# Decoder chain on GpSimd: slices of 32 features, products placed between the links, level masks on VectorE

## The chip, the core and the metric

One core of a Trainium2 chip runs the whole program. The metric is the device time in microseconds of one execution; 16 iterations of one loop follow a prologue. Engines: PE is TensorE, DVE is VectorE, ACT is ScalarE, POOL is GpSimd, SP is SyncE and issues DMAs.

## What is computed

Two decoder layers over x of (64, 128, 256): a gated delta-rule attention, cross attention and a mixture of 4 experts, then latent attention, cross attention and a mixture of 8 experts. What the change touches is the start of the first one, whose decays need a very exact sum over the features:

```python
log_decay = -exp(A_log) * softplus(einsum('btd,hd->bth', x, W_alpha) + dt_bias)   # x: normalised rows
cum = cumsum(log_decay, -1)
L_mask = tril(exp(tril(cum[..., :, None] - cum[..., None, :])))
M = tril(-(wk_scaled @ wk.T) * L_mask, -1)
A = solve_triangular(eye - M, eye, lower=True, unit_diagonal=True)   # per head, block of 128
```

The kernel forms the sum over 256 features as products with their rounding errors and adds them in a fixed order with an exact two-sum. It forms A by blockwise inversion in seven levels: at each level a mask picks the blocks of M that join two halves.

## The kernel before

**Tiling.** An iteration handles G = 4 sequences of 128 tokens, tokens on the 128 partitions; two heads (DH). `NIT` = 16 iterations run on each engine in a loop of its own, ordered by semaphores that count; the order on each engine is written out by hand.

**The chain on POOL.** The feature chain of the *next* iteration's rows (`xn_next`) is formed by `chain_products` (L394) and `chain_links` (L419). Features are cut in four slices of 64. Per slice come 22 products (128x256 elements each: high and low parts, their products and error terms, into `sp_p` and `sp_e`), then 16 rounds of 4 features (LANES). A round is eight small links on 128x32 elements, acc_a, acc_b, acc_c, acc_d, acc_c, acc_c, acc_c, acc_s, six of which wait for the link just before them; acc_d needs no wait and the acc_c behind it waits for an earlier one. `link` (L631) counts them in `chain_step`. One place for products serves all slices, so a slice's products start when the last slice's links are over.

**What else stands in POOL's order** (L627 to L682): among the products of slice 0 the twelve level masks (`lev`, L647, 128x512; from level 3 on each waits for the product W of two levels before), the residual add of xn0 (L652, `xin_used`, after it SP moves the next rows), 5 rounds, the bias add (L656), which waits for the layer norm's `xn`, a wait for DVE's root (`ref_step`), 11 rounds, slice 1, 5 rounds, the add of onb_row (L663), a wait for the router's gates (`g_w`), and all the rest. Before the last 8 rounds it waits for `x_norm`; then `chain_step` reaches CHAIN_READ and SP moves x_in to xn_next and loads the rows after next. The chain ends with `au` (L678). POOL then centres those rows (`centered`, L506), waits for `y_ready`, squares them and adds the first 16 of 32 groups of squares (`first_squares`, L523), and forms `decay_table` (L533), which the next iteration's MT needs.

**On DVE.** The loop (L1732) begins with two copies and the last 16 additions of squares (`exact_squares`, L1418), in pieces between the levels of the inversion (Um += U, L1823); then `exact_variance`. After attention(0) comes the mixture of 4 experts (e = 0 to 4), with the router and pieces of the exact normalisation of the rows after next in between, attention(1), attention(2), and the mixture of 8. In attention a unit u is a max over the scores (L1854) and a subtraction (L1858); ACT forms the exponential (L804), PE transposes and multiplies. The decay is worked out in steps of 8 to 10 numbers per partition (`decay_exponential`, parts 0 to 9, L1507): part 0 waits for `au`. Parts 0 to 4 (17 steps) stand before the third output block of attention(2) (b == 2, unit 17), parts 5 to 7 (10 steps) before the fourth, parts 8 and 9 after `xT_copy(5)`. At the end `first_level` (L1634) forms MT and the first level for the next iteration.

**The prologue** runs the chain of the first rows split: POOL forms all products (four places, `slice_pe`), DVE the links, and POOL then sums and normalises the second rows, waiting for DVE's root of them, which stands in DVE's links of slice 3 (L1710).

## Time and profile before

| | us |
|---|---|
| median of 3 runs (lowest, highest) | 5413.46 (5405.54, 5415.52) |
| the profiled execution, its span | 5405.82, 5403.9 |
| PE busy | 4731.9 (88%) |
| DVE busy | 4303.5 (80%) |
| POOL busy | 3938.4 (73%) |
| ACT busy | 2323.7 (43%) |
| one iteration (middle of the trace, 2525 to 2845 us) | 320.0, PE 293.4, DVE 255.3, POOL 236.0 |

Times in rows are us from the start of the span. A timeline row is start, duration, engine, line, what it writes from what, and in brackets the idle time of its engine before it with what ended that. `x5` merges five instructions. L635 is a helper: all links and products of the loop stand under it, L563 those of the prologue, L503 the row sums.

### The profile page before, as it was taken

Reading aid. Unit: us, or ns where it says so; the run is one execution under the profiler, and the core shown is the slowest. Engines: PE = TensorE matmul, PEld = TensorE weight load, DVE = VectorE, ACT = ScalarE, POOL = GpSimd, SP = SyncE. Lnnn points to the kernel's source line nnn. Section 1 sums busy time; section 2 is a strip of 40 time slices with the busy share of each in tenths; the row PEclk is TensorE's granted clock in tenths of the full one; section 3 lists DMA queues with packets and bytes.
Section 4 is the critical chain, followed back from the end, with each engine's and each line's share of the span. In section 5 each row is a group of like instructions: output and inputs, shape, how many; then the busy total and the mean of one; then the engine's idle time right before and its main releaser. Section 6 shows DMA issues by size and latency. Waiting matters only on the chain.

```text
span 5403.9 us, 105986 instructions
## 1 busy us (share of the span) xinstructions
PE 4731.9 (88%) x28362; PEld 3086.5 (57%) x28362; DVE 4303.5 (80%) x11377; ACT 2323.7 (43%) x4480; POOL 3938.4 (73%) x10789
## 2 busy tenths in 40 slices
PE   1089999999999999999999999998999999899999
PEld 0065656656565565656556565664656556565655
DVE  8878788787878877787877778777787887878788
ACT  0044444454444444443444544445444444444444
POOL 7478686777868678686767868676785867778686
PEclk7599999999999999999999999999999999999999
DMA  3000000000000000000000000000000000000000
GB/s 89 8 13 9 21 1 25 5 9 21 1 29 1 25 5 9 21 1 29 1 13 17 9 21 1 25 5 9 21 9 21 1 25 5 9 21 1 21 1 17
DMA packets 61894, 78.20 MB, mean 14 GB/s; under 512 B 11168, under 2 KB 53808, under 8 KB 61232
## 3 DMA queue, kind: packets, MB, share of 16 engines
q1 hardware_dynamic: 52784, 62.42, 3.6%
q10 hardware_dynamic: 8448, 8.39, 0.4%
q8 instruction: 240, 3.93, 0.3%
q14 instruction: 422, 3.46, 0.2%
HBM read 45.04 MB, written 8.46 MB: 10 GB/s over the span
## 4 chain that ended last, share of the span: by engine, by line
PE 33%; POOL 29%; DVE 21%; issue 11%; ACT 4%; POOLq 2%; DMA 0%; DVEq 0%; ACTq 0%; SPq 0%
POOL acc_c L635 11%; POOL arena L635 6%; PE bank L1331 3%; PE bank L1238 3%; POOL acc_a L635 3%; POOL acc_b L635 3%; POOL acc_s L635 3%; POOL sl_t L635 2%; PE bank L1191 2%; DVE arena L2088 2%; PE bank L1067 2%; POOLq L634 2%; PE bank L1074 2%; PE bank L1157 2%; PE bank L1143 2%
## 5 line engine op out<-in xcount | busy, mean ns | idle before, releaser
L1854 DVE TENSOR_REDUCE smax<-bank 128x4 f32<-128x512 f32 x768 | 525.2, 684 | 92.3 <-PE bank L1149 51.0
L817 ACT ACTIVATE arena<-bank 128x512 f32<-128x512 f32 x768 | 454.9, 592 | 249.4 <-PE bank L1157 243.7
L1858 DVE TENSOR_TENSOR arena<-bank,smax 128x512 f32<-128x512 f32 x768 | 531.2, 692 | 26.4
L1157 PE MATMUL bank<-ident,arena 128*128 128x128 f32 x3072 | 485.8, 281 | 43.0 <-ACT arena L804 25.7
L1238 PE MATMUL bank<-w,arena 128*128 128x512 f32 x1024 | 490.4, 610 | 14.0 <-DVE arena L1806 14.0
L1143 PE MATMUL bank<-arena 64*128 64x512 f32 x1536 | 440.2, 650 | 64.4 <-ACT arena L841 28.0
L1157 PEld LDWEIGHTS bank<-ident,arena 128*128 128x128 f32 x3072 | 346.9, 141 | 242.9 <-ACT arena L806 82.2
L1271 PE MATMUL bank<-w,arena 128*128 128x256 f32 x2048 | 454.1, 380 | 13.9 <-ACT arena L876 13.9
L804 ACT ACTIVATE arena<-arena,rstd 128x512 f32<-128x512 f32 x512 | 368.1, 719 | 197.9 <-DVE arena L1858 193.4
L1271 PEld LDWEIGHTS bank<-w,arena 128*128 128x128 f32 x2048 | 387.8, 190 | 90.3 <-issue 23.0
L635 POOL TENSOR_TENSOR acc_a<-acc_s,arena 128x32 f32<-128x32 f32 x1008 | 262.1, 260 | 175.4 <-DVE gate L1973 51.8
L876 ACT ACTIVATE arena<-bank,lnb,lng 128x512 f32<-128x512 f32 x256 | 197.3, 777 | 442.1 <-PE bank L1256 439.3
L1169 PE MATMUL bank<-arena 128*32 128x128 f32 x6144 | 327.5, 285 | 57.1 <-ACT arena L810 54.5
L949 PE MATMUL bank<-causal,identb 128*128 128x512 bf16 x658 | 158.5, 380 | 201.9 <-DVE y_nat L1596 198.9
L635 POOL TENSOR_TENSOR acc_c<-acc_a,acc_b 128x32 f32<-128x32 f32 x1008 | 265.7, 264 | 79.7
L635 POOL TENSOR_TENSOR acc_s<-acc_a,acc_c 128x32 f32<-128x32 f32 x1008 | 266.0, 264 | 78.9
L635 POOL TENSOR_TENSOR acc_c<-acc_c,arena 128x32 f32<-128x32 f32 x1008 | 264.4, 262 | 78.8
L635 POOL TENSOR_TENSOR acc_b<-acc_a,acc_s 128x32 f32<-128x32 f32 x1008 | 264.0, 262 | 78.8
L635 POOL TENSOR_TENSOR acc_c<-acc_c,acc_d 128x32 f32<-128x32 f32 x1008 | 262.5, 260 | 78.9
L503 POOL TENSOR_TENSOR arena<-arena 128x1024 f32<-128x1024 f32 x17 | 32.2, 1893 | 394.2 <-DVE y_nat L1596 394.1
L635 POOL TENSOR_TENSOR arena<-arena,sl_t 128x256 f32<-128x256 f32 x384 | 289.2, 753 | 27.6
L647 POOL TENSOR_TENSOR arena<-arena,levmask 128x512 f32<-128x512 f32 x192 | 239.8, 1275 | 65.6 <-DVE arena L1643 65.6
(437 smaller groups left out, 11962.0 us busy)
## 6 DMA issues: line engine op xcount, KB each, us to landing
arena<-in_x_dram SPq DMA_DIRECT2D x35, 512.0 KB, 3.6
xn_next<-arena SPq DMA_DIRECT2D x17, 512.0 KB, 2.9
arena<-cum_dram SPq DMA_DIRECT2D x17, 512.0 KB, 3.8
arena<-in_ctx_dram SPq DMA_DIRECT2D x16, 512.0 KB, 3.7
out_dram<-arena ACTq DMA_DIRECT2D x16, 512.0 KB, 3.1
xn<-xn_next SPq DMA_DIRECT2D x15, 512.0 KB, 3.0
w<-in_L_ffn_w_dram SPq DMA_DIRECT2D x8, 512.0 KB
w<-in_L_ffn_w_dram SPq DMA_DIRECT2D x1, 1024.0 KB
```

Source lines behind the costliest of these rows:

```text
L635: operation(*operands).then_inc(chain_step, 1)
L647: pool.tensor_tensor(heads(lev[:, l % 2, h, :]), heads(MT[:, h, :]), levmask[:, l, :].unsqueeze(1).broadcast_to([P, G, P]), ALU.mult).then ...
L804: act.activation(Ssb[:, v % 4], Ssb[:, v % 4], ACT.Exp, scale=rstd[:, v // 4:v // 4 + 1]).then_inc(S["p_exp"], 1)
L817: act.activation(PT[:, v % 2], bank[3 + v % 2][:, :].rearrange("p (h q) -> p h q", h=QH), ACT.Copy).then_inc(S["pt"], 1)
L876: act.activation(zT[:, e % 2, k, :], bank[4 + n % 2][:, :], ACT.Relu, scale=lng[:, e, k:k + 1], bias=lnb[:, e, k:k + 1]).then_inc(S["zT"], 1)
L1143: ins = mm(bank[S_BANKS[v % 4]][:, :], QT[rows, c, g * P:(g + 1) * P], KM[rows, g, min(c, chunks - 1)].rearrange("p h t -> p (h t)"), star ...
L1157: ins = tr(bank[3 + v % 2][:, j * P:(j + 1) * P], Ssb[:, v % 4, j, :], ident[:, :])
L1169: ins = mm(bank[5][2 * HD * j:2 * HD * (j + 1), (v % 4) * P:(v % 4 + 1) * P], V2[:, g, (v % 4) * QH + j, :], PT[:, v % 2, j, :], start=Tru ...
L1238: ins = mm(bank[g][:, :], xT[:, c, g * P:(g + 1) * P], w1_0[:, e, c, :], start=(c == 0), stop=(c == C - 1))
L1271: ins = mm(bank[6 + g // 2][:, (g % 2) * D:(g % 2 + 1) * D], zT[:, e % 2, k, g * P:(g + 1) * P], w2_0[:, e, k, :], start=(k == 0), stop=(k ...
L1854: dve.tensor_reduce(smax[:, u, :], sc, AX, ALU.max).then_inc(S["s_max"], 1)
L1858: dve.tensor_tensor(Ssb[:, u % 4], sc, smax[:, u, :].unsqueeze(2).broadcast_to([P, QH, P]), ALU.subtract).then_inc(S["s_sub"], 1)
```

## The change

Slices have 32 features, so there are eight, each with 22 products of 128x128 elements and 8 rounds. Two sets of product places (`sp`) alternate, and the products of slice j + 1 are issued one by one between the links of slice j, at three places of each round. Only the 22 products of slice 0 stand alone. Waits count links and products apart. The twelve level masks go to DVE: four and two copies at the start, the masks of level l + 2 behind the add of level l. The 16 additions of squares go from DVE to POOL, behind `decay_table` (`second_squares`). Parts 0 to 3 of the decay's exponential stand behind units 12 to 15 of attention(2), parts 4 and 5 before block 2, parts 6 to 8 before block 3. POOL's waits stand at other rounds. In the prologue POOL forms eight slices of products, DVE eight of links, with its inserted work at the same rounds as before.

```diff
-SLICE = 64
+SLICE = 32
-        sp_p = unit(24, 0, DH * G * SLICE).rearrange("p (h b d) -> p h b d", b=G, d=SLICE)
-        sp_e = unit(24, DH * G * SLICE, DH * G * SLICE).rearrange("p (h b d) -> p h b d", b=G, d=SLICE)
+        sp = [[half_slice(24, 2 * m), half_slice(24, 2 * m + 1)] for m in range(2)]
+        slice_pe = [[half_slice(u, 2 * m), half_slice(u, 2 * m + 1)] for u in (24, 7, 9, 0) for m in range(2)]
...
                 link(tt, acc_a[:, :, :], acc_s[:, :, :], pj, ALU.add)
+                if between:
+                    between()
                 link(tt, acc_b[:, :, :], acc_a[:, :, :], acc_s[:, :, :], ALU.subtract)
                 link(tt, acc_c[:, :, :], acc_a[:, :, :], acc_b[:, :, :], ALU.subtract)
                 link(tt, acc_d[:, :, :], pj, acc_b[:, :, :], ALU.subtract, known=True)
                 link(tt, acc_c[:, :, :], acc_s[:, :, :], acc_c[:, :, :], ALU.subtract, behind=1)
+                if between:
+                    between()
                 link(tt, acc_c[:, :, :], acc_c[:, :, :], acc_d[:, :, :], ALU.add)
                 link(tt, acc_c[:, :, :], acc_c[:, :, :], ej, ALU.add)
+                if between:
+                    between()
                 link(tt, acc_s[:, :, :], acc_a[:, :, :], acc_c[:, :, :], ALU.add)
...
+            def second_squares(it, a):
+                w8 = sq.rearrange("p b (k n) -> p b k n", n=32)
+                for k in range(16, 32):
+                    sum_link(it, a, pool.tensor_tensor, lan2[:, :, :], lan2[:, :, :], w8[:, :, :, k], ALU.add)
...
+                def counted(operation, operands, after):
+                    if after > 0:
+                        pool.wait_ge(chain_step, nth(it, CHAIN_STEPS, after))
+                    operation(*operands).then_inc(chain_step, 1)
+                    count["all"] += 1
+                def rounds(first, last):
+                    for n in range(first, last):
+                        j, k = divmod(n, SLICE // LANES)
+                        def next_product():
+                            if j + 1 < SLICES and count["next"] < PRODUCTS:
+                                chain_products(pool, product, src, j + 1, sp[(j + 1) % 2], count["next"], count["next"] + 1)
+                                count["next"] += 1
+                        if k == 0:
+                            count["next"] = 0
+                            count["link"] = count["product"] = count["all"]
+                        chain_links(pool, link, j, k, k + 1, sp[j % 2], next_product)
+                        if j == 0 and k + 1 == SLICE // LANES:
+                            next_product()
...
-                for l in range(1, LEVELS):
-                    chain_products(pool, link, src, 0, LEVEL_PRODUCTS[l - 1], LEVEL_PRODUCTS[l])
...
+                chain_products(pool, product, src, 0, sp[0])
+                rounds(0, INPUT_ROUND)
...
-                chain_links(pool, link, 0, 0, 5)
+                rounds(INPUT_ROUND, NORM_ROUND)
...
-                chain_links(pool, link, 0, 5, 16)
-                chain_products(pool, link, src, 1)
-                chain_links(pool, link, 1, 0, ROUTER_LINKS)
+                rounds(NORM_ROUND, ROUTER_ROUND)
...
-                chain_links(pool, link, 1, ROUTER_LINKS, 16)
...
+                rounds(ROUTER_ROUND, READ_ROUND)
                 pool.wait_ge(x_norm, nth(it, 1, 1, 2))
-                chain_links(pool, link, 3, 8, 16)
+                rounds(READ_ROUND, SLICES * SLICE // LANES)
...
                 decay_table(it, 1)
+                second_squares(it, 1)
...
-                xT_copy(0)
+                level_mask(1, 0)
                 wait("ctx_psum", 2)
                 dve.tensor_copy(ctxT[:, 1, :], bank[3][:, :]).then_inc(S["ctxT_dve"], 1)
-                dve.wait_ge(sum_step, nth(it, SUM_STEPS, SUM_STEPS))
-                exact_squares(16, 21)
+                level_mask(1, 1)
+                xT_copy(0)
+                for h in range(DH):
+                    level_mask(2, h)
...
+                    if l + 2 < LEVELS:
+                        for h in range(DH):
+                            level_mask(l + 2, h)
...
-                        exact_squares(21, 25)
...
-                        exact_squares(29, 32)
+                        dve.wait_ge(sum_step, nth(it, SUM_STEPS, SUM_STEPS))
                         exact_variance()
...
+                            if a_no == 2 and 12 <= u:
+                                decay_exponential(u - 12)
...
                             if a_no == 2 and b == 2:
-                                for part in range(5):
-                                    decay_exponential(part)
+                                decay_exponential(4)
+                                decay_exponential(5)
                             if a_no == 2 and b == 3:
-                                for part in range(5, 8):
+                                for part in range(6, 9):
                                     decay_exponential(part)
...
                 xT_copy(5)
-                decay_exponential(8)
...
+INPUT_ROUND = 6
+NORM_ROUND = 9
+ROUTER_ROUND = 25
+READ_ROUND = 58
-CHAIN_READ = 530
+CHAIN_READ = 640
-CHAIN_STEPS = 594
+CHAIN_STEPS = 682
```

## Rows read from the trace of the kernel before

**Rows 1.** the chain of work that ended last, share of the span by engine
```profile
PE 33%; POOL 29%; DVE 21%; issue 11%; ACT 4%; POOLq 2%; DMA 0%; DVEq 0%; ACTq 0%; SPq 0%
```

**Rows 2.** waits: who waited for whom, us in total, times, longest
```profile
POOL arena L503 <- DVE y_nat L1596: 394.1, 16, 26.7
```

**Rows 3.** line L1511, what ended DVE's idle time before it: us, times
```profile
  POOL au L678: 16.7, 13
```

**Rows 4.** timeline of POOL, the first link after the gates
```profile
2641.41 0.25 POOL L635 TENSOR_TENSOR acc_a<-acc_s,arena 128x32 f32<-128x32 f32 x1 [3.24 <-DVE gate L1973]
```

**Rows 5.** timeline of POOL, links from 2580 us, then 22 products, then links
```profile
2580.39 0.25 POOL L635 TENSOR_TENSOR acc_a<-acc_s,arena 128x32 f32<-128x32 f32 x1 [2.96 <-DVE row L1398]
...
2581.26 0.25 POOL L635 TENSOR_TENSOR acc_d<-arena,acc_b 128x32 f32<-128x32 f32 x1
2581.47 0.25 POOL L635 TENSOR_TENSOR acc_c<-acc_s,acc_c 128x32 f32<-128x32 f32 x1
...
2606.76 0.61 POOL L635 TENSOR_TENSOR sl_t<-xn_next,splitter 128x256 f32<-128x256 f32 x1
...
2623.88 0.26 POOL L635 TENSOR_TENSOR acc_a<-acc_s,arena 128x32 f32<-128x32 f32 x1
```

**Rows 6.** POOL by line and shape: count | busy us, mean ns | idle
```profile
L472 POOL TENSOR_TENSOR levmask<-arena 128x128 f32<-128x128 f32 x7 | 3.2, 453 | 0.6
...
L635 POOL TENSOR_TENSOR arena<-arena,sl_t 128x256 f32<-128x256 f32 x384 | 289.2, 753 | 27.6
...
L647 POOL TENSOR_TENSOR arena<-arena,levmask 128x512 f32<-128x512 f32 x192 | 239.8, 1275 | 65.6 <-DVE arena L1643 65.6
...
L503 POOL TENSOR_TENSOR lan<-lan,arena 128x32 f32<-128x32 f32 x238 | 64.3, 270 | 18.6
```

**Rows 7.** timeline at the start of an iteration
```profile
2517.89 0.61 POOL L635 TENSOR_TENSOR sl_t<-xn_next,splitter 128x256 f32<-128x256 f32 x1
...
2522.70 0.69 DVE L1641 TENSOR_TENSOR arena<-arena,levmask 128x512 f32<-128x512 f32 x1
...
2527.97 4.68 DVE L1425 TENSOR_TENSOR lan<-lan,arena 128x32 f32<-128x32 f32 x5
...
2532.78 1.29 DVE L1823 TENSOR_TENSOR arena<-arena,bank 128x512 f32<-128x512 f32 x2
...
2533.52 1.25 PE L1089 MATMUL bank<-ident,arena 128*128 128x128 f32 x8 [0.51 <-DVE arena L1823]
...
2575.09 2.35 POOL L656 TENSOR_TENSOR arena<-arena,bo_row 128x1024 f32<-128x1024 f32 x1 [8.20 <-DVE arena L1802]
```

**Rows 8.** timeline at the end of attention(2): start, us, engine, line [idle before]
```profile
2779.49 0.69 DVE L1854 TENSOR_REDUCE smax<-bank 128x4 f32<-128x512 f32 x1 [0.81 <-PE bank L1149]
...
2786.78 0.20 POOL L678 TENSOR_TENSOR au<-acc_a 128x8 f32<-128x8 f32 x1
...
2787.01 0.27 DVE L1511 TENSOR_TENSOR dec_t<-au,a_row 128x8 f32<-128x8 f32 x1 [0.86 <-POOL au L678]
...
2787.72 0.74 ACT L804 ACTIVATE arena<-arena,rstd 128x512 f32<-128x512 f32 x1
...
2788.80 0.66 PE L1178 MATMUL bank<-ident,arena 128*128 128x128 f32 x4
...
2790.82 0.26 DVE L1875 RECIPROCAL orec<-bank 128x16 f32<-128x16 f32 x1
```

**Rows 9.** timeline of DVE, three steps beside work of POOL
```profile
2635.99 2.21 DVE L1927 TENSOR_TENSOR arena<-arena,lt_mask 128x16 f32<-128x16 f32 x1
...
2685.90 1.10 DVE L1398 TENSOR_TENSOR arena<-arena 128x512 f32<-128x512 f32 x1
...
2714.16 0.48 DVE L1474 SCALAR_TENSOR_TENSOR arena<-arena,row 128x256 f32<-128x256 f32 x1
```

**Rows 10.** timeline of the prologue, DVE's first link and POOL's second quotient
```profile
70.83 0.65 DVE L1700 TENSOR_TENSOR acc_s<-arena 128x32 f32<-128x32 f32 x1 [6.95 <-POOL arena L563]
...
192.04 1.90 POOL L563 TENSOR_TENSOR arena<-arena,row 128x1024 f32<-128x1024 f32 x1 [42.81 <-DVE row L1398]
```

## What the change should do to the time

> **What bounds the kernel now.** The chain that ended last is shared: POOL 29%, PE 33%, DVE 21% [rows 1]. So I read next who waits for POOL. Of its 16 iterations (320 us each) POOL itself idles long, 394.1 us for y_nat [rows 2], which is slack: it has nothing to do until attention(2) has left its buffers. What it delivers late is `au`, the end of the feature chain: DVE stood idle for it 16.7 us in 13 places, 1.04 us per iteration [rows 3]. Before that, POOL waits 3.24 us for the gates [rows 4]. So the loop runs gates, 145 us of POOL, `au`, tail of attention(2); the path through PE and DVE is only about 1 us shorter. However fast POOL gets, that little is what an iteration can return there. The rest of the question is what moves onto DVE, and the prologue.
>
> **POOL's chain, step by step.** A round of eight links takes (2606.76 - 2580.39)/11 = 2.40 us: two steps of 0.21 us and six of 0.33 [rows 5]. The step from acc_d to the next acc_c has a wait on an earlier link and still takes 0.21, so a wait that is already met costs nothing; 0.12 us is what a link pays for waiting on the link just before it. A block of 22 products takes 2623.88 - 2606.76 = 17.1 us [rows 5]. For the half-size product the trace has a 128x128 tensor_tensor of 453 ns on POOL, against 753 ns for 128x256 [rows 6]; I take 0.46. Put between two dependent links it costs 0.21 + 0.41 - 0.33 = 0.29 us net (bounds: 0.21, if its start also hides, and 0.54, its whole length with a wait of its own of 0.08). All 176 instead of 88 products: 22 in one block at about 0.52 = 11.4 us, 154 between links at 0.29 = 45 us, together 56 against 68 us. The twelve level masks leave POOL: 12 x 1.25 = 15 us [rows 6]. Sixteen additions for the squares come, 16 x (0.27 + 0.08 for the wait) = 5.5 us [rows 6], behind `decay_table`.
>
> The waits between cut this into pieces. (1) Start to bias add: POOL comes to the chain at 2517.9 [rows 7]; squares 5.5, products 11.4, the round of one link, five rounds of 3.27, the residual add 2.4, three rounds 9.8 give 2563.4; with DVE's own masks in its way (12 x 0.5 us, first level 2) 2571. The bias add can't start before 2575.1 [rows 7], so all of this gain is idle time. The residual add is over at about 2562, before DVE asks for it at 2566. (2) From 2580.4 to the gates: 16 rounds x 2.40 + 44 x 0.29 = 51 us against 55.4; POOL waits some 4 us longer. (3) From the gates, 2641.4 [rows 4]: 39 rounds x 2.40 + 85 x 0.29 = 118 us, and 6 us of collisions as now (now 43 x 2.40 + 2 x 17.1 = 137.4 worked out, 145.1 measured): `au` at about 2767 instead of 2786.8 [rows 8]. x_norm, for which POOL waits in round 58, is written at the end of attention(1), about 2743, and POOL gets there at about 2750: no wait. move_next and load_x come with it, 7 us for both before `centered`, about as long as the 12 us that are left.
>
> **What that returns.** DVE now asks for `au` after unit 12, at 2780.9 (its max of that unit starts at 2779.49, 0.69 + 0.72 us [rows 8]): 14 us of slack. Of the decay steps (17 in 2790.82 - 2787.01 [rows 8], 0.21 us each) 13 move into units 12 to 15: 0.8 + 3 x 0.6 us. The last subtraction ends at 2787.8 instead of 2786.15, while its exponential starts at 2787.72 now [rows 8]: hidden but for 0.1 to 0.3. Behind them DVE has 8 steps instead of 17: it reaches the reciprocal at 2788.4 + 1.65 = 2790.05 instead of 2790.82, and PE has delivered by 2789.4 [rows 8]. That is 0.77 us, with the mean wait (1.04, here 0.86) **0.95 us** per iteration. After it PE and DVE take turns, nothing of POOL. The step that leaves the place behind xT_copy(5) (0.6 us) lies beside PE's expert matmuls: nothing.
>
> **Masks on DVE.** 12 x 0.69 us replace 16 squares of 0.66 to 1.2 (five in 4.68 [rows 7]): in 40 us, DVE isn't fuller. In level 1 the squares kept DVE until 2532.78 from adding U, which PE had ready at 2531.1; PE took its next transposes at 2533.52, having been free from 2532.9 [rows 7]: **-0.6 us**. In the later levels the two masks (1.4 us, waiting for nothing) and the decay product fit well into 5.9 us. But POOL used to stand still while DVE formed the first level, and now runs squares and products: three of its four ops on SBUF alone wait for a product each, about 0.2, **+0.6 us** on the path.
>
> **Two engines on one memory path.** This is the unknown term. A DVE gate op of 0.16 us took 2.21 us beside POOL's 2.37 us add; a subtraction of the masks' shape, which take 0.69 [rows 7], took 1.10 beside 128x256 products; a step of 0.48 us beside links took 0.48, nothing more [rows 9]. Products held DVE up, links did not. The product blocks stood at fixed places; now a quarter of the time until 2751 is products, each of half the length. On the path I count: mixture_norm 8 ops, **+0.5**; attention(1), where DVE runs without a gap, 8 ops, **+0.3**; small steps of the norms, **+0.2**; and e == 3, whose block goes, **-0.5** (DVE was 2.9 us longer there, but PE delivers only 0.5 us before). Together +0.5; bounds: -0.5 (no op waits) and +3 (20 ops on the path at 0.14, a third of those 0.41: the duty and length of the new products). The Trainium skill, SBUF — State Buffer, section "SBUF: two separate sides", says that the pair of ports is locked for the whole instruction and that the loser blocks fully. The 2.21 us agree; the 0.48 us beside links that run 0.25 of every 0.33 us do not. By that rule every POOL op would hold DVE, and the loop would lose nearer the upper bound.
>
> **Prologue.** DVE's chain begins when the first 22 products are there: 53.7 + 11.3 = 65.0 instead of 70.83 [rows 10]. Beside products it does two ops per POOL op; 16 rounds in 53.6 us now, and 37 in 85 us with the short ones. POOL's sums then end at 175 instead of 149, but it waited 42.81 us for DVE's root [rows 10], which comes at 184: **-7.9 us** (bounds -10 and 0). All behind it moves along.
>
> **Sum.** Per iteration -0.95 - 0.6 + 0.6 + 0.5 = -0.45; 16 x -0.45 - 7.9 = -15 us. The profiled execution took 5405.8 (span 5403.9), so 5391 by its own time; the median of the three runs is 5413.5, 0.14% above, and I give the time on its level: **5398 us**.
>
> **Rivals.** *Collisions are light* (0.13): as beside links, no DVE op waits. Then -0.95 - 0.6 - 0.5 = -2.05 per iteration, -33 - 8 us: 5372. For it: the 0.48 rows. *The tail gives nothing* (0.17): PE or ACT is as late as DVE, the added steps in units 12 to 15 eat the 0.95: +0.5 x 16 - 8: 5414. For it: the moved subtraction ends 0.1 us after the exponential's present start. *Collisions decide, slower* (0.14): DVE ops between 2517 and 2750 wait for interleaved products with +3 instead of +0.5 per iteration: -0.45 + 2.5 = +2.05, +33 - 8: 5438. It decides from 1.0 us of added waiting per iteration. For it: 1.10 against 0.69. *The products don't hide* (0.06): at 0.54 net each, `au` comes at 2787, DVE stands at unit 12 for 6.2 us of which 2 have slack: +4.2 x 16: 5465. It begins to hurt at 0.29 + 14/85 = 0.45 us net. Against it: the met wait at 0.21.
>
> **Chances.** My forecast 0.50, its own range 5385 to 5411. About 0.2% (11 us) is what a measurement of this kernel tells from no change. Faster: two thirds of the forecast, all of the first rival, 0.02 of the second: 0.48. Slower: most of the third and all of the fourth: 0.19. Same: 0.33. Range: 5372 to 5430, leaving out half of the third rival, the fourth and a rest below.
>
> **What would show it.** DVE's wait for `au` gone, POOL's last link at about -20 us against attention(2); rounds of 3.27 us with three products; POOL's waits for y_nat near 44 us per iteration, for the gates 7 and for the bias add larger; the add of U in level 1 directly behind PE; DVE's root in the prologue at 184. Wrong, if two-input DVE ops in attention(1) or mixture_norm are longer than 0.48 by more than 0.1 in the mean, if the first level takes over 1 us more, or if the tail between the last score and the reciprocal is not shorter.

## The result, and the profile after

| | before | after |
|---|---|---|
| median (lowest, highest), us | 5414.49 (5405.54, 5416.1) | 5361.07 (5358.8, 5361.5) |
| ratio of the medians, 95% interval | | 0.9903 (0.9888, 0.9918) |
| profiled execution, its span | 5405.82, 5403.9 | 5361.46, 5359.7 |
| mean granted clock of TensorE, of full speed | .954 | .961 |
| first iteration starts at | 281.7 | 274.2 |
| one iteration, mean of 16 | 319.86 | 317.56 |

The change makes the kernel 0.97% faster, 53 us. I had forecast 5398 us, with a range down to 5372: the direction was right, the size too small and the range too narrow.

The page of after, busy time by engine and the chain that ended last:

```profile
PE 4697.3 (88%) x28362; PEld 3072.0 (57%) x28362; DVE 4119.1 (77%) x11313; ACT 2322.5 (43%) x4480; POOL 3977.9 (74%) x12365
...
PE 62%; DVE 22%; issue 8%; ACT 6%; SPq 1%; POOL 1%; DVEq 0%; DMA 0%; ACTq 0%; POOLq 0%
```

POOL stood on the chain with 29% [rows 1] and has 1% of it now. PE executes the same 28362 matmuls in 34.6 us less (4731.9 before): the same work at a higher clock. That is the first sign of what the forecast had left out. The waits of after (who waited for whom, us in total, times, longest):

```profile
POOL arena L509 <- DVE y_nat L1622: 664.7, 16, 42.4
POOL acc_a L648 <- DVE gate L2011: 103.5, 16, 6.5
...
POOL arena L689 <- DVE arena L1828: 49.2, 16, 4.1
```

POOL waits 41.5 us per iteration for y_nat where it waited 24.6 [rows 2], and 6.5 for the gates where it waited 3.24 [rows 4]. Nobody waits for `au` any more; its last link comes 19.2 us earlier in the iteration. To see where the time went I took, in both traces, the start of some twenty instructions relative to the start of DVE's first level (L1639 in before, L1665 in after, where the forming of MT begins), and averaged over the 16 iterations. The last mixture norm is its last op, layer norm 5 its first add, attention(1) and attention(2) their first max over scores. Per stretch, after minus before, beside what the sum had said:

| stretch of an iteration | forecast, us | measured, us |
|---|---|---|
| start to attention(0): first level, inversion | 0.0 | -0.61 |
| to the last mixture norm: attention(0), router, experts | +0.2 | +2.0 |
| to the first score of attention(1) | 0.0 | -1.8 |
| attention(1) to attention(2) | +0.3 | +0.2 |
| attention(2) to layer norm 5 | -0.95 | -1.84 |
| mixture of 8 to the end | 0.0 | -0.2 |
| sum | -0.45 | -2.3 |

Two stretches that the forecast had at about nothing moved by 2 us in opposite directions, and the tail returned twice what it should.

**The tail: the clock.** PE's timeline around block 2 of attention(2), in two iterations of before (start, duration, engine and line, what it writes from what; in brackets its idle time before it), the seventh first, and then PE's busy time and granted clock (the column behind the count) in 8 us that hold the block:

```profile
2470.60 0.44 PE L1199 MATMUL bank<-ident,arena 128*128 128x128 f32 x2 [1.54 <-DVE arena L1877]
...
2471.32 1.36 PE L1191 MATMUL bank<-wo,arena 128*128 128x256 f32 x4
2472.48 1.06 PE L1178 MATMUL bank<-ident,arena 128*128 128x128 f32 x4
```

```profile
1509.52 0.44 PE L1199 MATMUL bank<-ident,arena 128*128 128x128 f32 x2 [0.34 <-DVE arena L1877]
...
1510.24 1.13 PE L1191 MATMUL bank<-wo,arena 128*128 128x256 f32 x4
1511.21 0.60 PE L1178 MATMUL bank<-ident,arena 128*128 128x128 f32 x4
```

```profile
2469.20:2477.20 8.00, 6.60 (x32) 0.79 0.01 3
```

```profile
1507.20:1515.20 8.00, 7.65 (x62) 1.00 0.02 5
```

The same iteration of after, PE's timeline and the window of all engines (PE, PEld, DVE, ACT, POOL, clock):

```profile
2449.35 0.44 PE L1225 MATMUL bank<-ident,arena 128*128 128x128 f32 x2 [0.47 <-DVE arena L1915]
...
2450.07 1.13 PE L1217 MATMUL bank<-wo,arena 128*128 128x256 f32 x4
2451.04 0.60 PE L1204 MATMUL bank<-ident,arena 128*128 128x128 f32 x4
```

```profile
2448.60:2456.60 8.00, 7.52 (x50) 4.88 (x45) 6.23 (x27) 2.51 (x7) 0.00 (x0) 1.00 0.01 4
```

Behind an idle stretch of 1.54 us four transposes take 1.06 us, behind 0.34 and 0.47 us they take 0.60. TensorE has fallen from its full 2.4 GHz to 1.2 GHz for part of the block. Over the 16 iterations of before PE's gap ahead of this block is between 0.34 and 2.81 us. The clock of the 8 us that hold the block is .79 in eight iterations, those with a gap of 1.5 us or more (one of 1.56 us kept 1.00), and 1.00 in the rest. In after the gap is 0.46 to 0.49 and the clock 1.00 in all 16. So the wait for `au` [rows 3] had a second price, which no wait row shows: the slower matmuls after it. The Trainium skill, TensorE: Matmul & The Clock Gate, section "Part 1: The HAM clock gate (the "warmup" mystery)", says that a monitor halves the array's clock when the engine has been idle; the rows agree that the clock falls behind idle time, and of the monitor they show nothing.

**The mixture: collisions lose 2 us, the clock gives 1.8 back.** DVE's groups by line and shape, count | busy us, mean ns | idle; first before, then after:

```profile
L1474 DVE SCALAR_TENSOR_TENSOR arena<-arena,row 128x256 f32<-128x256 f32 x272 | 139.6, 513 | 5.1
...
L1466 DVE TENSOR_SCALAR arena<-arena,row 128x256 f32<-128x256 f32 x68 | 37.0, 585 | 0.1
...
L1984 DVE SCALAR_TENSOR_TENSOR arena<-arena,rstd 128x256 f32<-128x256 f32 x64 | 27.8, 473 | 0.0
```

```profile
L1500 DVE SCALAR_TENSOR_TENSOR arena<-arena,row 128x256 f32<-128x256 f32 x272 | 154.4, 568 | 5.1
...
L2022 DVE SCALAR_TENSOR_TENSOR arena<-arena,rstd 128x256 f32<-128x256 f32 x64 | 33.3, 560 | 0.0
...
L1492 DVE TENSOR_SCALAR arena<-arena,row 128x256 f32<-128x256 f32 x68 | 23.4, 385 | 0.1
```

The ops that met a 17 us block of products got shorter without it (L1466 585 ns, L1492 385). They are the quotient behind expert 3, two per iteration, 378 instead of 821 ns, and what DVE saves there it spends waiting for PE (L2048, 53.9 us in total; the same op waited 2.4 us for PE in before); the two behind expert 1 didn't change (378 and 397 ns). Other ops got longer. The eight steps of the quotient's rest behind expert 1 (L1474, now L1500) take 576 instead of 495 ns in the mean, 0.65 us per iteration, and DVE's z of expert 2, for which PE waits, comes 1.0 us later. The last op of the mixture norm, L1984, has become L2022 and takes 560 instead of 473 ns, four times per iteration. PE's wait for z, before and then after:

```profile
PE bank L1256 <- DVE arena L1998: 36.6, 21, 2.2
```

```profile
PE bank L1282 <- DVE arena L2036: 52.6, 32, 2.2
```

What PE's clock did in the 20 us around the end of the mixture, the eighth and the seventh iteration, before and then after (busy us, clock):

```profile
2692.00:2712.00 20.00, 15.46 (x73) 0.91 0.01 2
2371.20:2391.20 20.00, 15.74 (x73) 0.89 0.01 2
```

```profile
2668.20:2688.20 20.00, 15.16 (x79) 1.00 0.00 1
2350.60:2370.60 20.00, 15.16 (x78) 0.97 0.01 1
```

The mean over the 16 iterations is .871 before and .974 after. PE's idle stretches there are not shorter in after (it stood 1.02 us before L1020 in the eighth iteration of before, and 1.32 us before the same transposes in after), so this is a gain whose cause I can't name; more below.

### The profile page after: what moved, and what is told of

Its sections match the earlier page's. It is cut to its first block, busy times and chain, and to the rows that moved or that the text cites. A ratio compares the mean times of both kernels' runs of the same rounds, so it can differ in the third digit from the quotient of the medians.

```text
span 5359.7 us, 108430 instructions
## 1 busy us (share of the span) xinstructions
PE 4697.3 (88%) x28362; PEld 3072.0 (57%) x28362; DVE 4119.1 (77%) x11313; ACT 2322.5 (43%) x4480; POOL 3977.9 (74%) x12365
## 4 chain that ended last, share of the span: by engine, by line
PE 62%; DVE 22%; issue 8%; ACT 6%; SPq 1%; POOL 1%; DVEq 0%; DMA 0%; ACTq 0%; POOLq 0%
PE bank L1264 7%; PE bank L1297 5%; PE bank L1357 5%; PE bank L1183 5%; PE bank L1169 4%; PE bank L1383 3%; PE bank L1195 3%; PE bank L1217 3%; PE bank L1093 3%; DVE smax L1890 3%; PE bank L1100 3%; DVE arena L1500 2%; PE bank L1282 2%; ACT arena L856 2%; PE bank L1175 2%
## 5 line engine op out<-in xcount | busy, mean ns | idle before, releaser
L648 POOL TENSOR_TENSOR acc_a<-acc_s,arena 128x32 f32<-128x32 f32 x1008 | 273.2, 271 | 225.9 <-DVE gate L2011 103.5
L1297 PEld LDWEIGHTS bank<-w,arena 128*128 128x128 f32 x2048 | 387.8, 190 | 90.3 <-issue 23.0
L648 POOL TENSOR_TENSOR arena<-arena,sl_t 128x128 f32<-128x128 f32 x768 | 361.3, 470 | 9.7
L648 POOL TENSOR_TENSOR acc_b<-acc_a,acc_s 128x32 f32<-128x32 f32 x1008 | 288.9, 287 | 10.0
L1264 PEld LDWEIGHTS bank<-w,arena 128*128 128x128 f32 x1024 | 185.6, 198 | 170.9 <-issue 153.6
L509 POOL TENSOR_TENSOR lan<-lan,arena 128x32 f32<-128x32 f32 (+1 forms) x748 | 237.6, 318 | 57.2
```

The lines of the kernel that those rows point to most:

```text
L509: operation(*operands).then_inc(sum_step, 1)
L648: operation(*operands).then_inc(chain_step, 1)
L1264: ins = mm(bank[g][:, :], xT[:, c, g * P:(g + 1) * P], w1_0[:, e, c, :], start=(c == 0), stop=(c == C - 1))
L1297: ins = mm(bank[6 + g // 2][:, (g % 2) * D:(g % 2 + 1) * D], zT[:, e % 2, k, g * P:(g + 1) * P], w2_0[:, e, k, :], start=(k == 0), stop=(k ...
```

## The experiments

Each run was timed beside the kernel before. Offsets are means over 16 iterations from the start of the iteration, as above; "clock" is the granted clock of a stretch, a mean over 16 windows (170 to 190 us and 268 to 276 us of each iteration). `keep_busy(n, bank)` issues n matmuls whose result nobody reads.

| kernel | median, us | last mixture norm | attention(1) | `au` | layer norm 5 | iteration | clock, end of mixture | clock, block 2 |
|---|---|---|---|---|---|---|---|---|
| before | 5414.5 | 176.06 | 189.53 | 264.85 | 274.04 | 319.86 | .871 | .893 |
| after | 5361.1 | 177.44 | 189.09 | 245.62 | 271.94 | 317.56 | .974 | 1.00 |
| b_fill_tail | 5393.2 | 175.88 | 189.65 | 264.88 | 273.63 | 319.13 | .867 | 1.00 |
| b_fill_mix | 5421.3 | 176.07 | 187.53 | 264.77 | 274.57 | 320.99 | 1.00 | .751 |
| m_only | 5391.1 | 175.67 | 189.20 | 262.51 | 274.01 | 320.15 | .882 | .864 |
| a_oldtail | 5360.3 | 177.47 | 189.23 | 245.85 | 271.54 | 317.34 | .975 | 1.00 |
| m_router | 5392.9 | 175.93 | 189.27 | 255.28 | 272.97 | 319.04 | .883 | .933 |
| m_router_c | 5330.1 | 175.72 | 187.26 | 254.78 | 269.60 | 315.07 | .995 | 1.00 |
| a_quiet | 5344.0 | 175.07 | 187.33 | 234.97 | 270.64 | 315.73 | .951 | 1.00 |
| b_short | 5398.3 | 175.77 | 190.70 | 262.34 | 274.95 | 320.92 | .796 | .956 |
| a_rebal | 5369.9 | 175.65 | 189.30 | 246.21 | 272.26 | 317.75 | .876 | 1.00 |
| a_fill_end | 5373.0 | 178.19 | 190.11 | 246.72 | 272.94 | 318.70 | .963 | 1.00 |
| a_late | 5360.0 | 177.31 | 189.42 | 264.04 | 272.13 | 317.61 | .961 | .987 |
| a_late2 | 5404.1 | 177.45 | 189.11 | 265.25 | 274.20 | 319.84 | .981 | .853 |
| a_mixfill | 5361.05 | 177.46 | 188.92 | 245.64 | 271.79 | 317.50 | .990 | 1.00 |
| a_rebal_fill | 5321.6 | 176.16 | 187.70 | 246.67 | 270.43 | 315.02 | 1.00 | 1.00 |
| a_rebal_fill2 | 5306.9 | 174.65 | 186.11 | 245.97 | 269.02 | 314.14 | .990 | 1.00 |
| m_best | 5320.2 | 174.69 | 186.16 | 254.68 | 268.69 | 314.72 | .984 | 1.00 |

The offsets and clocks are those of the one profiled execution, the median that of all runs. After, a_oldtail, a_late and a_mixfill agree with themselves within 2 to 4 us; before, m_only and b_short scatter by 11, 37 and 41 us, so for these the trace of one execution is a weaker witness.

### The clock in the kernel before

**b_fill_tail**: the kernel before, with six such matmuls where PE would stand idle ahead of block 2.

```diff
+                        if a_no == 2 and u == QUADS + 2:
+                            keep_busy(6, 2)
```

> The kernel before, with six matmuls without a use (128x512 bf16, 0.22 us each) put on PE where it stands idle in the tail of attention(2), before the transposes that wait for DVE's third output block. Theory C (TensorE's clock): in 8 of the 16 iterations of before the granted clock is 0.79 in the 8 us behind that idle time, and matmuls there last 1.91 us instead of 1.03; with the gap filled the clock stays at 1.00 and about 1.3 us come back in each of the 8: -10 us, about 5404. Theory P (path): only the decay steps on DVE and the wait for au count; matmuls put into an idle stretch return nothing: within 3 us of before. Both: the wait for au stays, 1 us per iteration.

Measured: ratio 0.9962 (0.9949, 0.9975), 17 us against the runs of before beside it, 21 against the 5414.5 of the table. `au` comes when it did (+0.04), DVE waits for it as before, and the clock of block 2 is 1.00 in all 16 iterations instead of .893. That alone is worth about 1 us per iteration. The clock is a cost of its own, beside the wait.

**b_fill_mix**: the same remedy at the end of the mixture.

```diff
-MIX_FILL = 14
+MIX_FILL = 18
...
+                keep_busy(4, 2)
```

> The kernel before, with 4 more of the useless matmuls between the two halves of the last mixture norm (18 instead of 14) and 4 behind the second half, where PE waits for xT. Theory C: the two latent matmul groups behind them, which last 3.2 to 3.8 us instead of 1.95 in most iterations of before (granted clock 0.74 to 0.91), go at full clock: 1.2 us per iteration, -19 us, about 5395. Theory P: no change, or some us more, since PE comes to the second half later: 5410 to 5425.

Measured: ratio 1.0016 (1.0008, 1.0025), slower by 7 to 11 us, though the clock there rose from .871 to 1.00 and attention(1) starts 2.00 us earlier. DVE's wait for `au` in the seventh iteration, PE's gap behind it, and PE's windows at block 2 and at the end of the mixture (eighth iteration):

```profile
2472.93 0.27 DVE L1512 TENSOR_TENSOR dec_t<-au,a_row 128x8 f32<-128x8 f32 x1 [2.75 <-POOL au L678]
```

```profile
2477.49 0.44 PE L1199 MATMUL bank<-ident,arena 128*128 128x128 f32 x2 [3.21 <-DVE arena L1878]
```

```profile
2476.00:2484.00 8.00, 6.51 (x32) 0.79 0.01 2
```

```profile
2698.80:2718.80 20.00, 16.59 (x84) 1.00 0.01 2
```

`au` stays at 264.77, since it hangs on the gates 145.9 us before it and on nothing between. The 2 us turn into a longer wait and then into a slow clock in every iteration. This is why before can't keep a gain that is made ahead of `au`, and why the same gain at the mixture counts in after: there `au` comes 19 us earlier.

### What of the change does it

**m_only**: the level masks on DVE and the squares on POOL, slices of 64 and product blocks kept, nine rounds before the bias add.

```diff
-                for l in range(1, LEVELS):
-                    chain_products(pool, link, src, 0, LEVEL_PRODUCTS[l - 1], LEVEL_PRODUCTS[l])
...
+                chain_products(pool, link, src, 0)
+                chain_links(pool, link, 0, 0, 4)
...
+                    if l + 2 < LEVELS:
+                        for h in range(DH):
+                            level_mask(l + 2, h)
```

> The kernel before with only the masks on DVE and the 16 squares on POOL; the chain stays at slices of 64 with its products in blocks, and nine rounds instead of five stand before the bias add. The decay steps stay where they were. au then comes some 9.6 us earlier, before DVE asks for it. Theory A (the gain of the change is the end of the wait for au and of what it does to the clock, plus the level inversion): -0.64 -1.04 and 0.65 for the clock per iteration, -2.3, about -37 us: 5377. Theory B (the finer, interleaved products are what brings it, because the blocks of 17 us held DVE up): only the level inversion and the wait, -1.7 per iteration at most, and less if the block now meets other steps of the mixture: -10 to -27 us, 5387 to 5404.

Measured: ratio 0.9962 (0.995, 0.9974), runs from 5379 to 5416; the profiled one, 5410.4, is among its slowest. The median lies in theory B's range, but theory A wasn't tried, since `au` hardly came earlier. The last mixture norm stays at -0.39 against before, where after has +1.38: the collisions come with the interleaved products. `au` gains only 2.3 us, tied to the gates as before (145.75 us behind them): the time POOL was given ahead of the gates it spends waiting for them.

**a_oldtail**: after, with the decay steps back at their old places.

```diff
-                            if a_no == 2 and 12 <= u:
-                                decay_exponential(u - 12)
...
+                                for part in range(5):
+                                    decay_exponential(part)
```

> The kernel after with the decay steps where they stood before: 17 ahead of the third output block, 10 ahead of the fourth, the rest behind the norm; au is early all the same. Theory of the prediction: the place of the steps is worth 0.77 us per iteration, +12 us against after: 5373. Theory C: PE then stands idle for 17 x 0.21 = 3.5 us of DVE's steps, the clock falls behind it as in before, +0.8 +1.3 us in each iteration: +34 us, 5395. Theory W (only the wait counted): the steps are hidden as well there, 5361.

Measured: ratio 0.9905 (0.9891, 0.992), after's 5361.1 against 5360.3. As theory W said, once `au` is early, the place of the steps is worth nothing. My 0.77 us for moving 13 of them was wrong.

**m_router**: m_only, with four more rounds before the wait for the gates.

```diff
-ROUTER_LINKS = 5
+ROUTER_LINKS = 9
```

> As the kernel with only masks and squares exchanged, and four more rounds (9 instead of 5 of slice 1) stand on POOL before its wait for the gates; products still in blocks of 22 at 128x256. In the first version au stayed tied to the gates (146 us behind them) and came only 2.3 us earlier. Theory L (the loop gates, POOL, au bounds the iteration, and only what shortens it behind the gates counts): au now comes 9.6 us earlier still, before DVE asks for it, and the loop runs as PE and DVE allow: about 317.5 to 318.5 us per iteration, 5365 to 5380. Theory B (the gain needs the fine products, since blocks of 17 us hold DVE up): au is early too, but the time stays above 5385.

Measured: ratio 0.9965 (0.9953, 0.9977), 5392.9, where theory B had put it, but with another reason than the blocks. `au` is 9.6 us earlier than before and DVE never waits for it; still the clock at block 2 falls in 5 of 16 iterations. In all five one of DVE's decay steps takes over 1.8 us; in the thirteenth iteration it is the first:

```profile
4368.24 1.89 POOL L503 TENSOR_TENSOR arena<-arena,row 128x1024 f32<-128x1024 f32 x1
4368.30 1.86 DVE L1511 TENSOR_TENSOR dec_t<-au,a_row 128x8 f32<-128x8 f32 x1
...
4370.19 0.17 DVE L1512 SCALAR_TENSOR_TENSOR dec_t<-dec_t 128x8 f32<-128x8 f32 x1
```

POOL, early by 10 us, arrives with its 128x1024 subtraction at the place where DVE works on 8 elements per partition: that step takes 1.86 us here and 0.16 in eight of the 16 iterations, and PE stands idle 1.75 to 1.82 us in these five. In three more iterations a step is as long and PE idle for 1.72 us, and the clock stays at 1.00. The Trainium skill, SBUF — State Buffer, section "SBUF: two separate sides", says that a DVE operation with two SBUF inputs and a GpSimd operation that reads SBUF exclude each other for a whole instruction. These rows agree.

**m_router_c**: m_router, with POOL held before that subtraction until the reciprocal of the last block.

```diff
                 if a:
+                    pool.wait_ge(S["o_rec"], at(it, "o_rec", 12))
```

> Masks and squares exchanged, products in blocks, 9 and 9 rounds ahead (5393 before), and POOL's subtraction of the row mean (128x1024, 1.9 us) held back until DVE is past the last output block of attention(2). In the run without this wait the first of DVE's decay steps took 1.86 us beside it instead of 0.17, and PE stood idle 1.75 us ahead of the third block in 7 of 16 iterations. Theory S (that one operation cost it the tail): the step takes 0.2 us, PE's idle time there is 0.65 us or less, the clock in the tail 1.00: 0.6 to 1.2 us per iteration, 5374 to 5383. Theory B (blocks of products elsewhere cost it): within 5 us of 5393.

Measured: ratio 0.9854 (0.9838, 0.987), 5330.1 us: 31 us faster than after, with blocks of 128x256 products and slices of 64. PE's windows at the end of the mixture and at block 2, eighth iteration:

```profile
2656.60:2676.60 20.00, 15.41 (x76) 1.00 0.01 2
2754.60:2762.60 8.00, 7.21 (x35) 1.00 0.00 0
```

Its last mixture norm lies 1.7 us ahead of after's, and both clocks are nearly full (.995 and 1.00). `au` at 254.8 instead of 245.6 costs nothing. The run gained far more than the 5374 to 5383 expected of the one wait: of its 4.0 us per iteration against m_router 1.5 lie in the tail, 1.8 at the end of the mixture, where the clock rose from .883 to .995 though the edit touches nothing there, and 0.6 behind layer norm 5. That the held subtraction mends the tail is shown; why the clock at the mixture rose is not.

### What the interleaved products cost

**a_quiet**: after; between rounds 25 and 45 each product works on 8 of its 32 columns, so that part of the feature products is left out.

```diff
+                    if small:
+                        operands = [o[:, :, 0:8] for o in operands[:3]] + [operands[3]]
```

> The kernel after, in which the products that stand between the links from the gates to the last mixture norm (rounds 25 to 45) work on 8 of the 32 columns only (128x32 elements), so that the chain keeps its instructions and nearly its length, but its result is not the decay any more. Theory K (collisions on the path): the products cost 2.0 us per iteration between the gates and the last mixture norm (the marker moved from -0.6 to +1.4 us against before); without them PE's wait for DVE's z falls from 52.6 to under 37 us in all and -1.2 to -2.0 us per iteration return: 5330 to 5342. Theory M (the mixture waits elsewhere anyhow, for instance for PE's own matmuls, and the clock takes it back): within 8 us of after, 5353 to 5369.

Measured: ratio 0.9872 (0.9857, 0.9887), 17 us less than after, 2 us short of theory K's range. PE's wait for z is back at what it was in before:

```profile
PE bank L1284 <- DVE arena L2038: 37.4, 16, 2.4
```

The last mixture norm comes 2.36 us earlier than in after: the products cost there what the table of stretches shows. Of this 0.6 us is lost again until attention(1), where the clock is .951 instead of .974, and the iteration keeps 1.83. The difference is spread over many small steps: most of the roots' steps on 128x2 and 128x4 and of the quotient's on 128x256 take 0.04 to 0.2 us more in after than in a_quiet. `au` comes 10.7 us earlier too, but a_late, below, shows that such a lead is worth nothing.

**b_short** leaves out the last round of POOL's chain in before, so the features of that round are missing from the sum.

```diff
-                chain_links(pool, link, 3, 8, 16)
+                chain_links(pool, link, 3, 8, 15)
```

> The kernel before, in which POOL leaves out its last round of eight links (the sum lacks four features, so the decay is not the reference's); au comes 2.4 us earlier, nothing else changes. Theory T (the tail is worth its wait and the clock behind it): DVE's wait of 1.04 us is gone, PE's idle time ahead of the third block falls below 0.7 us, the granted clock in the 8 us behind it is 1.00 in all iterations instead of 0.89 in the mean: 1.04 + 0.8 us, -29 us, 5381. Theory W (the wait alone): -17 us, 5394. Theory P (the path of PE and DVE is only a little shorter, and the gain comes back at the mixture): -0 to -8 us.

Measured: ratio 0.9971 (0.9957, 0.9984), runs from 5383 to 5423. In the profiled run, the slowest, `au` is 2.5 us earlier, DVE doesn't wait for it, and the clock of block 2 rises from .893 to .956, but that at the end of the mixture is .796, and the iteration takes 320.92. The median, 16 us under before, is theory W's, but with runs 41 us apart and a profile of the slowest it doesn't separate the theories: `au` did what was expected, and in that execution another place took more back.

### How early `au` has to be

**a_late** and **a_late2**: a_oldtail with 58 and 62 additional links behind the last one, whose results nobody reads.

```diff
+                for _ in range(58):
+                    link(pool.tensor_tensor, acc_b[:, :, :], acc_s[:, :, :], acc_s[:, :, :], ALU.add)
```

> The kernel after with the decay steps at their old place (which changed nothing: 5360), and 58 small additions of 128x32 behind the last link on POOL, whose result nobody reads; they take 58 x 0.33 = 19 us and put au back to where it stands in before, 265 us into the iteration, with everything else of the change in place. Theory T (the tail is worth its wait and the clock behind it): DVE waits for au 1 to 2.5 us again, PE stands idle 1.3 to 2.5 us ahead of the third block, the granted clock behind it falls to 0.79 in about half of the iterations or more, +2.0 to +2.6 us per iteration: 5392 to 5402. Theory W (only the wait itself, as the prediction summed it): +1.0 us per iteration, 5377.

> As the kernel with late au, with 62 instead of 58 additions behind the last link. With 58 of them au came at 264.0 us of the iteration, DVE waited 0.2 to 0.4 us, and the time was that of after; the one iteration in which DVE waited 1.21 us and PE stood idle 1.5 us was also the one with a granted clock of 0.79 behind it. Now au comes 1.3 us later, DVE waits about 1.7 us. Theory T: PE is idle 1.9 us ahead of the third block, the clock behind it falls to 0.79 in nearly all iterations, 1.3 + 0.8 us each: +34 us, 5394. Theory W: 1.3 us, +21 us, 5381.

Measured: a_late 5360.0, ratio 0.9904 (0.9889, 0.9919), the time of after, with `au` 18.4 us later than in after. a_late2, with `au` another 1.2 us later: 5404.1, ratio 0.9984 (0.9976, 0.9993), 44 us more, 10 beyond theory T's 5394. The sixth iteration of a_late, DVE's wait and PE's gap:

```profile
2128.38 0.27 DVE L1539 TENSOR_TENSOR dec_t<-au,a_row 128x8 f32<-128x8 f32 x1 [0.38 <-POOL au L705]
```

```profile
2132.79 0.44 PE L1227 MATMUL bank<-ident,arena 128*128 128x128 f32 x2 [0.68 <-DVE arena L1915]
```

The same of a_late2, and PE's windows at block 2 in the fourth, fifth and sixth:

```profile
2138.18 0.27 DVE L1539 TENSOR_TENSOR dec_t<-au,a_row 128x8 f32<-128x8 f32 x1 [1.62 <-POOL au L705]
```

```profile
2142.58 0.46 PE L1227 MATMUL bank<-ident,arena 128*128 128x128 f32 x2 [1.92 <-DVE arena L1915]
```

```profile
1501.60:1509.60 8.00, 6.22 (x31) 0.79 0.01 2
1822.80:1830.80 8.00, 6.78 (x47) 1.00 0.01 4
2140.70:2148.70 8.00, 6.11 (x30) 0.79 0.02 4
```

In 11 iterations the wait is 1.62, the gap 1.92 and the clock .79; in the other five the gap is at most 1.21 and the clock stays at 1.00. The iteration grows by 2.2 us for 1.2 us of POOL. And a_late, whose `au` is only 0.8 us earlier than before's (264.04 against 264.85), has after's whole gain. In this pair of kernels, of the 19 us that the change takes off POOL's chain the first one counts, and counts nearly double; the rest is worth nothing.

### The end of the mixture, and a better version

**a_rebal**: after, with half of the `exact_rest` steps moved from expert 1 to expert 2, difference and last to expert 3.

```diff
-                        for part in range(4):
+                        for part in range(2):
...
+                        for part in range(2, 4):
...
+                        exact_difference(0)
+                        exact_last(0)
```

> The kernel after, with DVE's exact steps spread differently over the mixture of 4: four instead of eight of the exact_rest steps behind expert 1, the other four behind expert 2, difference and last behind expert 3, where DVE waits 2.9 us for PE. Nothing on POOL changes. Theory K: DVE at expert 1 is what the mixture waits for since the products lie beside it (PE waits 1.03 us for z there): about -1.0 us per iteration, 5345. Rival: the wait moves to expert 2 or 3, or the clock falls at another place: 5355 to 5365.

Measured: ratio 0.9916 (0.9902, 0.9929), 5369.9: 9 us slower than after. The last mixture norm is 1.79 us earlier, as it should be, and attention(1) starts 0.2 us later. PE's window in the eighth iteration:

```profile
2669.10:2689.10 20.00, 15.26 (x67) 0.88 0.01 2
```

The clock that after had at .974 has fallen to .876, and takes back all of it, as the rival had said (5 us above its range).

**a_mixfill**, **a_rebal_fill** and **a_rebal_fill2**: after with useless matmuls at the end of the mixture, a_rebal with the same, and this with ten more behind the router.

```diff
-MIX_FILL = 14
+MIX_FILL = 19
...
+                keep_busy(4, 2)
...
-                keep_busy(8, 4)
+                keep_busy(18, 4)
```

> The kernel after with only the useless matmuls in the mixture's last two idle stretches (19 instead of 14, and 4), DVE's exact steps as in after. It splits the gain of 39 us that both edits gave together. Theory A (the two need each other): the clock there is at 0.974 already, so the filling alone returns 0.4 us per iteration, 5352 to 5358. Theory F (the filling is what brought it): 5325 to 5335.

> The kernel after with DVE's exact steps spread as in the run before (which brought the last mixture norm 1.8 us forward and lost all of it to a granted clock of 0.88 instead of 0.97 in the 20 us behind), and useless matmuls in PE's two idle stretches there (19 instead of 14, and 4). Theory C: the clock stays at 1.00 in these 20 us, and both gains stand: -2 us per iteration, 5330. Rival: the clock falls at the next weak stretch instead (tail of attention(2), or the mixture of 8), as it did with the stretch before the mixture of 8 filled: 5355 to 5370.

> As the run before, and ten more useless matmuls (18 instead of 8) where PE waits 2.2 us for DVE's first z of the mixture of 4; the granted clock in the 26 us around it is 0.93 to 0.95. Theory C: -0.7 to -1.5 us per iteration more, 5310 to 5320. Rival: DVE's router bounds this stretch, PE's faster matmuls only wait longer at expert 1: as the run before.

Measured: a_mixfill 5361.05, ratio 0.9903 (0.9888, 0.9917); a_rebal_fill 5321.6, 0.9833 (0.982, 0.9847); a_rebal_fill2 5306.9, 0.9806 (0.9792, 0.9819). Filling alone gives nothing, moving the steps alone costs 9 us, both together give 39: DVE's steps and PE's clock each hide what the other is worth. The window of the fastest, eighth iteration:

```profile
2643.60:2663.60 20.00, 16.30 (x71) 1.00 0.00 1
```

**a_fill_end**: after with seven fillers before the mixture of 8, where after's clock is .85, and the matmuls of expert 0 among those of the router.

```diff
+                                keep_busy(3, 2)
...
+                keep_busy(4, 2)
```

> The kernel after, with seven useless matmuls in PE's two idle stretches (0.79 and 0.88 us) ahead of the mixture of 8, and the first expert's matmul group put into the middle of the 16 router matmuls of 8 columns. Theory C (clock): in every iteration of after the granted clock is 0.85 in the 23 us behind these stretches, with matmuls of 0.6 instead of 0.43 us; if it stays up, -2 to -3.4 us per iteration, 5307 to 5330. Rival: the drop comes whatever PE does in the gaps, or DVE's gates bound this stretch: within 8 us of after.

Measured: ratio 0.9922 (0.9909, 0.9936), 5373.0. PE's windows in the eighth iteration, 276 to 299 us after its start, after and a_fill_end:

```profile
2774.20:2797.20 23.00, 21.34 (x65) 0.85 0.00 0
```

```profile
2779.80:2802.80 23.00, 21.07 (x75) 1.00 0.00 0
```

The clock rose to 1.00 in these 23 us and the iteration is 1.1 us longer. From layer norm 5 to the end of the iteration it takes 45.8 us, after 45.6: the added matmuls and a lower clock behind them (.96 instead of 1.00 in the mean from 299 us to the end) cost what the higher one gave. A further 0.6 us is lost before attention(0), where five of the 16 iterations are 2 us late and the clock of the first 30 us is .974 instead of .993. Which of the two edits does it, the fillers or the moved group, no run separates.

**m_best**: m_router_c with the moved steps and the fillers (18, where a_rebal_fill2 has 19 in the norm), that is nearly a_rebal_fill2 with product blocks instead of interleaved products.

```diff
-MIX_FILL = 14
+MIX_FILL = 18
...
+                if a:
+                    pool.wait_ge(S["o_rec"], at(it, "o_rec", 12))
```

> Masks and squares exchanged, products in blocks of 64 features, POOL's subtraction held back (5330), together with the spread exact steps and the filled stretches of the best run so far (5307). Theory S (fine products bring nothing in the loop, only their 7.5 us of the prologue): the loop is at least as fast as with them, about 314 us per iteration or less: 5300 to 5315. Theory B (they are needed once the rest is filled): 5320 or more.

Measured: 5320.2, ratio 0.9822 (0.981, 0.9835). Its iteration takes 314.72 us where a_rebal_fill2 has 314.14, and it starts the loop at 281.9 instead of 273.0. The time is at theory B's bound and outside theory S's range, but 8.9 of the 13 us to a_rebal_fill2 are the prologue. In the loop the finer products bring 0.6 us per iteration or nothing; their clear gain is the prologue.

## Why the prediction was wrong

**The balance.** 5398 less 16 x 1.85 us (-2.30 measured, -0.45 forecast) plus 0.4 of the prologue is 5369. That is above the 5361 measured. The other 8 us are the step from the profiled execution to the median, which I carried over: after's profiled run lies at its median, before's lay 7.7 to 9 us under its own.

**Failed: the tail, -0.95, measured -1.84.** The step that failed is "the mean wait (1.04, here 0.86)" as the price of the wait. Its length was right; that the decay steps are moved adds nothing to it (a_oldtail): the missing 0.86 us alone gives 2789.96 for the reciprocal where the sum had 2790.05. What I had left out is the clock. The forecast priced the wait with the wait's own length; a_late2 shows 1.2 us of it costing 2.2, b_fill_tail some 1 us per iteration for the clock alone. What would have shown it was in the trace of before: the windows at block 2, .79 in half of the iterations, and the same four transposes in 1.06 and 0.60 us ([rows 8] has them at 0.66).

**Failed: collisions between gates and mixture norm, +0.2, measured +2.0.** The mechanism was named, and its bound of +3 for the loop held; the size was wrong. I counted eight ops of mixture_norm on the path, but z of expert 2 was already 1.0 us later than before: the steps behind the earlier experts count too. a_quiet confirms the price, 2.36 us. None of the three signs of being wrong showed it: two-input ops beside products took up to 0.56 us in mixture_norm and 0.57 in attention(1) in the mean, which is 0.08 and 0.09 above 0.48 where the sign asked for 0.1, the first level took no longer, and the tail did get shorter.

**Missing: the end of the mixture, 0, measured -1.8.** It is a clock again, .871 to .974. The forecast had no term for TensorE's clock anywhere. Without the two gains of clock, 1.8 here and 0.8 in the tail, an iteration would have come out at +0.3, three quarters of a microsecond above the forecast. Why the clock stays up in after is open. The idle stretches there are equal or longer in after, so their length doesn't explain it. a_rebal falls back to .876 with four of DVE's steps moved, and m_router_c rises to .995 with an edit elsewhere. What the runs settle is that it is worth about 1.8 us at the start of attention(1) (b_fill_mix -2.0 against before, a_rebal_fill -1.6 against a_rebal).

**Failed: the first level, +0.6, measured 0.** DVE's first level in after:

```profile
2498.87 0.69 DVE L1667 TENSOR_TENSOR arena<-arena,levmask 128x512 f32<-128x512 f32 x1
...
2500.93 0.72 DVE L1667 TENSOR_TENSOR arena<-arena,levmask 128x512 f32<-128x512 f32 x1
2501.68 0.69 DVE L1669 TENSOR_TENSOR arena<-arena,ident 128x512 f32<-128x512 f32 x1
```

The ops take 0.69 to 0.72, as in [rows 7]: POOL adds its squares (128x32) beside them and reaches its products, at 2501.83, only when the level is nearly formed.

**Right.** The add of U: it starts 1.5 us earlier in its iteration, and 0.61 of -0.6 remain at attention(0). Attention(1): +0.2 of +0.3. POOL's chain: `au` -19.2 of -20; the waits for y_nat 41.5 of 44 and for the gates 6.5 of 7. A round with three products, forecast 3.27, in POOL's timeline from acc_a to acc_a, 3.26:

```profile
2559.16 0.25 POOL L648 TENSOR_TENSOR acc_a<-acc_s,arena 128x32 f32<-128x32 f32 x1
2559.36 0.45 POOL L648 TENSOR_TENSOR arena<-arena 128x128 f32<-128x128 f32 x1
...
2562.42 0.25 POOL L648 TENSOR_TENSOR acc_a<-acc_s,arena 128x32 f32<-128x32 f32 x1
```

The prologue: -7.5 of -7.9 us, with DVE's chain at 66.1 (forecast 65.0) and its root, which POOL waits for, at 184.0 (forecast 184):

```profile
184.01 1.90 POOL L575 TENSOR_TENSOR arena<-arena,row 128x1024 f32<-128x1024 f32 x1 [9.15 <-DVE row L1424]
```

**A miss without weight.** I expected a longer wait of POOL before the bias add. It is 49.2 us in total and was 131.7: the rounds before it use the time. The bias add itself starts 0.6 us earlier, with level inversion.

**The rivals.** The light collisions (5372) came nearest, for a wrong reason: collisions were heavier than forecast, not lighter. That the tail gives nothing and that the products don't hide: both are refuted. That collisions decide is refuted in the time, 5438, but not in its mechanism: the collisions cost 1.8 us more per iteration than the sum had, past the 1.0 from which the rival said that they decide, and it is the clock, which neither the forecast nor a rival had, that gave this back.

## What to carry to other kernels

Price a wait on TensorE's path twice, by its length and by the granted clock of the windows behind it, and compare the same instruction in iterations with and without the gap. Ask how much of a lead is needed before building one: here POOL had to be 1 us earlier, not 19. And when an engine's work is spread finely to be finished sooner, what it meets on the way can cost more than its lead is worth: blocks of products, with one long operation held back, were 31 us faster than after.

## What the runs showed of the hardware

- Ahead of block 2, in before, after, a_late and a_late2, an idle stretch of PE of up to 1.36 us never lowered the granted clock; of those from 1.50 to 1.94 us all but one (1.56) did, and all of 2.3 us and more. In m_router three of 1.72 us kept it and five of 1.75 to 1.82 us lost it; in m_only three of 1.69 us lost it and three of 1.73 and 1.74 us kept it, so the length of the gap alone doesn't decide. At the lower level the four transposes took 1.06 instead of 0.60 us.
- Useless matmuls in such a gap kept the clock at 1.00 (b_fill_tail, b_fill_mix). What that brought differed by place: 17 to 21 us less in b_fill_tail and 48 less from a_rebal to a_rebal_fill, nothing in a_mixfill, and in b_fill_mix (+7 us) and a_fill_end (+12) it was lost again further on.
- A step of DVE on 8 elements per partition took 1.86 us beside a GpSimd subtraction of 1.89 us. Beside links of 0.25 us and products of 0.46 us a step of 473 ns took 560 in the mean.
